# What GpSimd waits for between its gathers in a recommender tower: landings of its own gathers, or look-ups on TensorE

## What is computed

```
e = jnp.stack([tbl_0[ids[:, 0]], ..., tbl_31[ids[:, 31]]], axis=1)      # 2048 x 32 x 16
row, col = _pair_indices(32)                                            # 496 pairs
z = jnp.sum(e[:, row, :] * e[:, col, :], axis=2)
h = jnp.concatenate([z, dense_ctx], axis=1)                             # 2048 x 512
h = jnp.maximum(h @ W_top1 + b_top1, 0.0)                               # 512 -> 512
h = jnp.maximum(h @ W_top2 + b_top2, 0.0)                               # 512 -> 256
y = h @ W_top3                                                          # 256 -> 1
```

## Time and profile before

| | |
|---|---|
| median of 3 runs | 370.39 us (370.32 to 371.34) |
| the profiled execution: its own time | 366.74 us |
| its span, first to last instruction | 364.9 us |
| TensorE busy | 288.4 us (79%) |
| VectorE busy | 274.6 us (75%) |
| GpSimd busy, 240 gathers of 0.94 us | 228.2 us (63%) |
| ScalarE busy | 132.3 us (36%) |
| mean granted TensorE clock | 0.869 |

### The profile page before, as it was taken

How to read it: one execution, slowest core, us unless ns; L and a number is a source line. 1 busy time by engine, 2 the same in 40 slices (tenths; PEclk the granted TensorE clock), 3 DMA queues, 4 the chain that set the end, 5 groups by cost and what they waited for, 6 DMA issues and landing times.

```text
span 364.9 us, 4524 instructions
## 1 busy us (share of the span) xinstructions
PE 288.4 (79%) x1711; PEld 253.3 (69%) x1711; DVE 274.6 (75%) x314; ACT 132.3 (36%) x250; POOL 228.2 (63%) x250
## 2 busy tenths in 40 slices
PE   0767948597969888897959698595976959689897
PEld 0456938496958886796849587494955949478695
DVE  7359699969794979788775958859397595968762
ACT  3554542435252433425242521435233352202322
POOL 6457665667666666765657666567665667666750
PEclk9985869699987989898969969698796988969999
DMA  6680020202020020202020120202002010010000
GB/s 143 194 285 7 6 68 7 68 6 70 5 69 5 6 70 6 67 8 67 5 69 6 13 63 6 67 8 57 16 7 67 5 9 5 7 9 5 6 7 1
DMA packets 19042, 14.60 MB, mean 40 GB/s; under 512 B 9727, under 2 KB 16461, under 8 KB 19022
## 3 DMA queue, kind: packets, MB, share of 16 engines
q1 hardware_dynamic: 10284, 11.69, 10.1%
q0 software_dynamic: 7680, 1.98, 7.1%
q10 hardware_dynamic: 1058, 0.66, 0.6%
HBM read 14.24 MB, written 0.08 MB: 39 GB/s over the span
## 4 chain that ended last, share of the span: by engine, by line
POOL 31%; PE 27%; issue 20%; DVE 15%; DMA 4%; ACT 1%; SPq 1%; POOLq 0%; ACTq 0%
POOL emb L383 31%; PE bank L640 8%; PE bank L658 6%; PE bank L687 6%; DVE prod L485 4%; DVE z_last L522 4%; DVE prod L494 3%; PE bank L698 2%; PE bank L636 2%; DMA emb<-tbl,idx 2%; DVE emb L475 2%; DMA gids<-small_ids_f 1%; DMA ids_flat<-small_ids 1%; PE bank L797 1%; DVE mask L453 1%
## 5 line engine op out<-in xcount | busy, mean ns | idle before, releaser
L383 POOL DMA_INDIRECT emb<-tbl,idx x240 | 226.9, 946 | 123.6 <-issue 63.9
L494 DVE TENSOR_TENSOR prod<-emb,bank 128x1904 f32<-128x1904 f32 (+5 forms) x51 | 94.4, 1852 | 43.5 <-DMA emb<-tbl,idx 43.5
L640 PE MATMUL bank<-turned_tab,onehot 125*128 125x160 f32 (+1 forms) x544 | 102.2, 330 | 0.0
L640 PEld LDWEIGHTS bank<-turned_tab,onehot 125*128 125x128 f32 x544 | 95.0, 224 | 6.5
L658 PE MATMUL bank<-ident,prod 128*128 128x128 f32 x528 | 73.1, 298 | 0.0
L658 PEld LDWEIGHTS bank<-ident,prod 128*128 128x128 f32 x528 | 71.5, 200 | 0.7
L522 DVE TENSOR_REDUCE z_last<-prod 128x150 f32<-128x2400 f32 (+3 forms) x32 | 66.8, 2086 | 1.1
L475 DVE TENSOR_REDUCE emb<-bank 128x48 f32<-128x480 f32 (+2 forms) x96 | 53.1, 585 | 15.1 <-PE bank L640 14.0
L687 PE MATMUL bank<-zT,w_sb 128*128 128x256 f32 (+1 forms) x256 | 61.4, 388 | 0.7 <-ACT zT L893 0.7
L636 PE MATMUL bank<-far_ten,named_ten 100*128 100x480 bf16 (+1 forms) x64 | 26.2, 410 | 41.9 <-DVE emb L475 36.5
L687 PEld LDWEIGHTS bank<-zT,w_sb 128*128 128x128 f32 x256 | 48.8, 207 | 6.5 <-ACT zT L893 0.9
(11 more groups left out here) (68 smaller groups left out, 121.3 us busy)
## 6 DMA issues: line engine op xcount, KB each, us to landing
gids<-small_ids_f SPq DMA_DIRECT2D x16, 544.0 KB, 3.9
emb<-tbl,idx POOLq DMA_INDIRECT x240, 2.4
w_sb<-w SPq DMA_DIRECT2D x1, 1024.0 KB
w_sb<-w SPq DMA_DIRECT2D x1, 512.0 KB
tab<-tbl SPq DMA_DIRECT2D x7, 56.0 KB
tab<-tbl SPq DMA_DIRECT2D x5, 70.0 KB
tab<-tbl ACTq DMA_DIRECT2D x5, 70.0 KB
z_last<-dense SPq DMA_DIRECT2D x16, 8.0 KB, 1.7
```

What stands on the lines that cost most here:

```text
L383: nc.gpsimd.indirect_dma_start(emb[:, t, at:at + D], None, tables[f], bass.IndirectOffsetOnAxis(ap=idx[:, t, f:f + 1], axis=0)).then_inc(d ...
L494: return nc.vector.tensor_tensor(prod[:, at * D:(at + n * a) * D].rearrange("p (j i d) -> p j i d", j=n, d=D), strided(emb_at(t, PLACES[g] ...
L640: mm = nc.tensor.matmul(look, onehot[:, place, i, :], turned_tab[:, CAND_AT[i] * D:CAND_AT[i + 1] * D], start=False, stop=(i == first + n ...
```

## The change

GpSimd no longer waits for landings, and SyncE no longer waits for GpSimd's gathers. The 240 gathers are taken as 48 rows of five, three rows for each tile. Behind each row GpSimd waits for `looked`: for round 5 of tile t behind the first row of tile t, for round 1 of tile t+1 behind the second, and for round 3 of tile t+1 behind the third. That is so from tile 8 on. In the first eight tiles the wait is for an older look-up: 4 rows older in tiles 0 and 1, then 3, 2 and 1 rows older for each two tiles. Where that lies ahead of the first window, or beyond tile 15, there is no wait. The waits for `made` stay.

```diff
--- before.py
+++ after.py
@@ -50,11 +50,10 @@
 
 
 GROUPS = [7, 5, 3]
-N_GATHERS = (TILES - 1) * (F - S)
 GROUP_AT = [S + sum(GROUPS[:g]) for g in range(len(GROUPS) + 1)]
 
-ROW_FROM = 3
-ROW_ENDS = [k for k in range(N_GATHERS) if k % (F - S) in (6, F - S - 1)]
+RUN = 5
+LEAD = 4
 
 SHIFTS = (S - 1) // 2
 CIRCLES = [(GROUPS[0] - 1) // 2, (GROUPS[1] - 1) // 2, 0]
@@ -252,9 +251,6 @@
         GROUP_STEPS = [GROUP0_STEP, GROUP1_STEP, BANK_STEP]
         STEPS = 7
 
-        def landings(t, g, i):
-            return 16 * (t // 2 * GROUPS[g] + i + 1)
-
         COPIES = 3
         LAST_TILE = TILES - 1
 
@@ -307,14 +303,6 @@
             def load_dense(t):
                 sp.dma_start(z_last[:, t % 2, N_SUMS:N_SUMS + N_DENSE], dense_v[:, t, :]
                              ).then_inc(dense_loaded[t % 2], 16)
-
-            def wait_for_row(gather):
-
-                end = min((k for k in ROW_ENDS if k >= gather), default=None)
-                if gather >= 0 and end is not None:
-                    tile, place = end // (F - S), end % (F - S) + S
-                    g = max(g for g in range(len(GROUPS)) if GROUP_AT[g] <= place)
-                    sp.wait_ge(landed[g][tile % 2], landings(tile, g, place - GROUP_AT[g]))
 
             sp.wait_ge(groups_steps, 4)
             sp.dma_start(scratch.rearrange("(p x) -> p x", p=P), groups_f16[:].rearrange("p f n -> p (f n)")
@@ -339,7 +327,6 @@
 
                 if t + 1 < TILES:
                     sp.wait_ge(distance_made, stretches_done(t - 1, len(STRETCHES) - 1))
-                    wait_for_row((t - 3) * (F - S) + ROW_FROM)
                     load_gids(t + 1)
                 sp.wait_ge(summed, chunks_done(t - 2, CHUNKS - 1))
                 load_dense(t)
@@ -363,6 +350,14 @@
             pool.wait_ge(ident_zeroed, 1)
             nc.gpsimd.affine_select(out=ident[:], in_=ident[:], compare_op=ALU.not_equal, fill=1.0, base=0,
                                     pattern=[[-1, P]], channel_multiplier=1).then_inc(ident_ready, 1)
+
+            def wait_for_look_ups(row):
+
+                third = row - 2 - max(0, LEAD - row // 6)
+                window, part = divmod(third, 3)
+                tile, r = ((window + 1, 3), (window + 1, 5), (window + 2, 1))[part]
+                if window >= 0 and tile < TILES:
+                    pool.wait_ge(looked, rounds_done(tile, r))
 
             pool.wait_ge(first_ids_loaded, 16)
             for t in range(TILES):
@@ -384,8 +379,9 @@
                             emb[:, t, at:at + D], None, tables[f],
                             bass.IndirectOffsetOnAxis(ap=idx[:, t, f:f + 1], axis=0)
                         ).then_inc(done, 16)
-                        if t * (F - S) + GROUP_AT[g] + i - S in ROW_ENDS:
-                            pool.wait_ge(done, landings(t, g, i))
+                        place = GROUP_AT[g] + i - S
+                        if place % RUN == RUN - 1 and (t, place) != (LAST_TILE, F - S - 1):
+                            wait_for_look_ups((F - S) // RUN * t + place // RUN)
 
         @block.vector
         def _(dve):
```

## The result

| | before | after |
|---|---|---|
| median of four runs | 370.36 us (369.7 to 371.3) | 342.3 us (three of 341.6 to 342.7, one of 347.3) |
| ratio | | 0.923, 95% interval 0.920 to 0.927 |
| the profiled execution | 366.74 us | 341.6 us |
| its span | 364.9 us | 339.8 us |
| mean granted TensorE clock | 0.869 | 0.92 |

What follows compares the result with a forecast made beforehand. The prediction took GpSimd's gather loop with its landing waits to bound windows 7 to 13. Span 364.9 - 17.2 + 0.2 = 347.9 us, so the median 370.39 - 17.0 = 353.4 us, range 350 to 358.5.

Steps and rivals of the forecast that it cites:

- The landing waits were the bound: Windows 7 to 13 run at GpSimd's pace; without landing waits its loop falls from 22.0 to 18.7 us a tile.
- rival C: GpSimd is held by something else, too many gathers under way; loop stays about 22 us, time 370; chance 0.04.
- rival B: Look-ups release gathers too late; VectorE waits about 1 us for group 1 in four odd windows; 357; chance 0.12.
- the 3.6 us spare in odd windows: Group 1's gathers land 3.1 us into an odd window, VectorE asks at 6.7; the least spare of all.
- D: Each unmet wait makes GpSimd drain and restart, at least 1.4 us each; slower, 377; chance 0.03.
- SyncE's wait: Transfers of ids lose a wait for a gather of tile t-3; the dense load ahead still holds them; 0.
- the undisturbed pace: Windows 7 to 13 at the pace of windows 2 to 6, 18.49 odd and 20.68 even: 136.0 us, 17.2 less.
- rival A: TensorE's clock rises too with shorter gaps; even windows win 1.3 us more and the tail 1; 351; chance 0.12.
- nothing is won before window 7: No window before window 7 waits for a gather, so the early windows gain nothing.
- The start itself: Two or three gathers move into the loading of tables and weights; costs 0.2 us, bounded by 0 and 1.
- The last two windows: Windows 14 and 15 are limited by TensorE and stay at 46.9 us; gain 0, 1 us to either side.
- if that part stays: The median's 3.65 us above the profiled execution, unexplained by the trace, was assumed to remain in the changed kernel.

Runs made afterwards that it cites:

- one_landing: The kernel before without the landing wait behind a tile's 7th gather, SyncE's wait moved to the next row end; on a slow chip 491.6 us, 1.166.
- before_no_sp_wait: The kernel before with SyncE's wait for a gather's landing taken out, GpSimd's landing waits kept; on slow chips 425.7 us against 428.0, 1.003.

## Why the prediction was right or wrong

**The landing waits were the bound: right.** VectorE's waits for gathers are gone where below 8 us were forecast, and GpSimd's remaining waits are ended by look-ups. The pitch of gathers stayed at 1.25 us, so rival C is refuted. VectorE never waits for group 1, so rival B too: the 3.6 us spare in odd windows were enough. Met waits cost nothing and unmet ones no restart, so D is refuted. SyncE's wait was worth nothing, by its timeline. All this is read from one trace of each kernel; no experiment ran where the 28 us were won.

**The sum was too small by 11 us.** By spans, 364.9 - 339.8 = 25.1 us were won, and 17.0 were forecast. Where they and the rest of the 28 us lie:

- *Windows 7 to 13, "the undisturbed pace": 136.0 forecast, 131.1 measured.* The even ones took 21.45, 18.59 and 18.64 us, a mean of 19.56 instead of 20.68 (3.4 us); the odd ones a mean of 18.1 instead of 18.49 (1.5 us). This is the step that failed. Windows 2 to 6 before were free of waits for gathers, and I took that for undisturbed. But windows 2 and 4 ran at a clock of 0.84, and that was a disturbance too: with the clock at 1.00 an even window is 18.6 us long and an odd one, at best, 16.9. The prediction had the rows in hand, compared window 9 with window 3, and left it at rival A with 1.3 us for the even windows where 3.4 were to be had.
- *Windows before 7, "nothing is won before window 7": 4 us were.* Window 7 starts at 160.84 instead of 164.81. The largest single part is the first window, in which VectorE waits for no gather in either kernel:

```profile
25.02:49.07 24.05, 16.90 (x111) 15.67 (x111) 20.93 (x32) 12.53 (x20) 14.49 (x15) 0.78 0.09 13
```

```profile
25.19:46.55 21.36, 14.67 (x111) 13.57 (x111) 20.68 (x32) 12.53 (x20) 16.18 (x18) 0.92 0.13 21
```

  The first row is of before, the second of after: 2.7 us shorter, TensorE busy 2.2 us less for the same 111 matmuls, clock 0.92 instead of 0.78. The landing waits that fall into it held GpSimd alone. Of the windows behind it two give back 1.0 and 0.6 us (windows 1 and 2) and two win 1.4 and 1.7 (4 and 6, TensorE's clock 0.84 and 0.92 before, 0.91 and 1.00 after), none of them with a wait of VectorE for a gather. So this may be one execution's luck with the clock as much as the change; the profiles can't tell. The start itself cost 0.17 us (25.19 instead of 25.02), as the 0.2 us in the sum.
- *The last two windows: 46.9 forecast, 47.9 measured*, within the 1 us given.
- *The part of the median above the profiled execution, 3.65 us, "if that part stays".* It didn't: 342.3 - 341.6 = 0.7 us. That is 3 of the 11 us. Why the profiled execution of before was the faster one stays open, as in the prediction.

Together: 17.0 + 4.2 (early windows, the forecast 0.2 among it) + 4.9 - 1.0 + 2.9 = 28.0 us.

**Rival A was the right mechanism with a wrong size.** It gave 351, and 342.3 came. Its other ground, that the pauses for gathers make bursts start cold, agrees with the traces in part: in windows 8 and 9 before, TensorE stood still for 2.09 and 1.50 us ahead of its usual pause of 2.4 to 2.6 us, and neither window was over 0.85; after, it is 0.21 us, and in windows 7 to 13 only one is under 0.91. (In windows 10 to 14 before, the extra pause is 1.46 to 3.07 us and the clock 0.84 or 0.85.) But window 8 after, with 0.21 us, is at 0.84 too. So the traces show that the long extra pause and a low clock go together, not that its absence gives a high one. And the experiments that were to show it ran on chips where a higher clock didn't shorten the time. That the 4.9 us come from the clock is shown: from windows 2 to 6 before to windows 7 to 13 after, TensorE's busy time for the same matmuls falls by a mean of 1.17 us in an even window and 0.40 in an odd one, and their length by 1.12 and 0.39. That the change is what raised the clock is argued.

**The blind spot was what closely packed gathers do to the other engines on a slow chip.** There the change is worth 1%, and it is the waits for look-ups that save it from being 18 to 20% slower. The prediction costed these waits only as a risk. Where 370 us were measured, runs of 75 and 90 gathers go unbroken in the changed kernel and no wait of TensorE's matmuls, ScalarE or VectorE is put down to "issue" or "remote"; whether the look-up waits are worth anything there, no run shows.

## What to carry to other kernels

Before windows that wait for nothing are taken as a kernel's undisturbed pace, compare TensorE's busy time for the same matmuls between them: where it differs, the granted clock is a wait of its own, and the pace to forecast with is that of the windows at full clock, as the upper end of the gain at least. A wait that only slows an engine down can be what keeps the others fed: on the slow chips taking waits away from between the gathers cost 17 to 20%, and pauses that make a gap of 1.5 us behind each five won 11.5%. So vary how the work of such an engine is spread, not only how much it waits, and measure on more than one chip before a wait is called useless.

## What the runs showed of the hardware that was not expected

- The kernel before took 370 us at first and 421 to 440 us later, on four chips. The changed kernel was profiled on both kinds: spans of 339.8 and 418.3 us with nearly the same busy times (TensorE 277.4 and 298.7 us at clocks of 0.920 and 0.837, VectorE 274.0 and 273.8). The rest is idle time.
- There, in one_landing, TensorE goes on in steps of 0.7 us or twice that from 12.0 us behind the start of an unbroken run of gathers until some 2.5 us behind its end (173.10 to 182.25 against a run from 161.07 to 179.7). With gathers in sevens and eights, 1.5 to 1.7 us between them, the same steps came as well (before_no_sp_wait, 90.56 to 108.35).
- Gaps behind each five gathers shorten the time there: of 1.5 us to 0.885 of the kernel before, without any wait for look-ups; of 1.25 us, with those waits, from 0.992 to 0.905; of 0.8 us, without them, from 1.175 to 1.198 down to 1.089.
- A met semaphore wait on GpSimd costs nothing: with 240 of them the gathers still follow each other at 1.25 us, and the time is 418.0 us instead of 417.5.
- Two windows with the same pauses of 0.21 and 2.57 us ran at a clock of 0.84 and of 1.00; eight matmuls take 3.48 us in the one and 1.89 us in the other.
